# Two square roots of a cross-attention kernel, moved from ScalarE's function to a Newton iteration on VectorE

## The reference

```python
def _l2norm(x, axis=-1):
    n = jnp.sqrt(jnp.sum(x * x, axis=axis, keepdims=True))
    return x / jnp.maximum(n, EPS)                      # EPS = 1e-12
q, k_t, v_t = heads(hidden_states @ W_q), heads(text_ehs @ W_k), heads(text_ehs @ W_v)
probs_t = jax.nn.softmax(jnp.einsum('bhsd,bhtd->bhst', q, k_t) * attn_scale, axis=-1)
text_out = jnp.einsum('bhst,bhtd->bhsd', probs_t, v_t)
attn_scores = jnp.einsum('bhsd,bhnd->bhsn', q, k_ip) * attn_scale
qsem = _l2norm(jnp.einsum('bhst,bte->bhse', probs_t, text_ehs))
ip_n = _l2norm(ip_ehs)
sem = jnp.einsum('bhse,bne->bhsn', qsem, ip_n)
probs_ip = jax.nn.softmax(attn_scores + SEM_SCALE * sem, axis=-1) * spatial_mask[None, None, :, None]
ip_out = jnp.einsum('bhsn,bhnd->bhsd', probs_ip, v_ip)
out = (text_out + ip_out) @ W_out + b_out + residual
```

## Time and profile before

| | before |
|---|---|
| median of 3 runs | 3430.9 us (3430.57 to 3434.68) |
| the profiled execution | 3429.41 us |
| its span | 3427.6 us |
| TensorE, matmuls | 3332.5 us busy, 97% |
| VectorE | 1994.7 us, 58% |
| ScalarE | 1832.7 us, 53% |
| GpSimd | 1089.9 us, 32% |
| mean granted TensorE clock | 0.992 |

### The profile page before, as it was taken

One profiled execution on the slowest core, in us unless ns is written; L12 is line 12 of the kernel. 1 busy time (PEld: TensorE's weight loads), 2 busy tenths in 40 slices (PEclk: granted clock), 3 DMA queues, 4 the chain that ended last, 5 costly groups with the idle time before them and its releaser, 6 DMA issues.

```text
span 3427.6 us, 65589 instructions
## 1 busy us (share of the span) xinstructions
PE 3332.5 (97%) x24736; PEld 2893.1 (84%) x24736; DVE 1994.7 (58%) x5517; ACT 1832.7 (53%) x4006; POOL 1089.9 (32%) x932
## 2 busy tenths in 40 slices
PE   6999999999999999999999999999999999999978
PEld 3888988887888888888888888888888898989755
DVE  4444455556656566565656556665565556555577
ACT  2333343455555555555655555555565556555678
POOL 2111001234332333333433332333423322322368
PEclk8999999999999999999999999999999999999999
DMA  6333823333367332233347422323326532222242
GB/s 185 103 92 71 98 53 92 81 83 83 86 83 101 78 73 68 75 92 82 91 72 72 98 73 68 78 71 106 87 71 75 67 57 49 63 49 53 46 86 54
DMA packets 648781, 271.28 MB, mean 79 GB/s; under 512 B 479666, under 2 KB 599426, under 8 KB 648468
## 3 DMA queue, kind: packets, MB, share of 16 engines
q1 hardware_dynamic: 648468, 267.10, 37.9%
HBM read 187.97 MB, written 79.04 MB: 78 GB/s over the span
## 4 chain that ended last, share of the span: by engine, by line
PE 88%; DVE 5%; ACT 2%; POOL 1%; issue 1%; SPq 1%; DMA 1%; POOLq 0%; ACTq 0%; DVEq 0%
PE acc L1144 9%; PE acc L1137 9%; PE acc L1140 8%; PE acc L1139 8%; PE acc L1145 8%; PE acc L1138 7%; PE score L1104 4%; PE score L1188 4%; PE spare L1188 4%; PE score L1106 4%; PE av L1175 3%; PE av L1179 3%; PE spare L1229 2%; PE spare L1278 2%; PE score L1229 2%; PE score L1278 2%
## 5 line engine op out<-in xcount | busy, mean ns | idle before, releaser
L1355 ACT ACTIVATE prob<-score 128x512 f32<-128x512 f32 x1219 | 729.0, 598 | 1182.5 <-PE score L1106 1177.5
L1775 POOL TENSOR_TENSOR prob_lo<-prob,prob_hi 128x512 fp32r<-128x512 f32 x624 | 812.2, 1305 | 1472.1 <-ACT prob_hi L1358 1471.6
L1137 PE MATMUL acc<-tok_v,prob_hi 128*128 128x300 f32 x2240 | 908.1, 405 | 0.9 <-issue 0.9
L1139 PE MATMUL acc<-tok_lo,prob_hi 128*128 128x256 f32 (+1 forms) x2560 | 760.0, 297 | 0.0
L1144 PE MATMUL acc<-tok_v,prob_lo 128*128 128x278 f32 (+1 forms) x2560 | 745.6, 291 | 0.0
L1358 ACT ACTIVATE prob_hi<-score 128x512 fp32r<-128x512 f32 x1219 | 726.1, 596 | 0.0
L1140 PE MATMUL acc<-tok_lo,prob_hi 128*128 128x256 f32 (+1 forms) x2560 | 719.1, 281 | 0.0
L1145 PE MATMUL acc<-tok_v,prob_lo 128*128 128x256 f32 (+1 forms) x2560 | 717.9, 280 | 0.0
L1138 PE MATMUL acc<-tok_v,prob_hi 128*128 128x256 f32 x2240 | 627.7, 280 | 0.0
L1140 PEld LDWEIGHTS acc<-tok_lo,prob_hi 128*128 128x128 f32 (+1 forms) x2560 | 483.7, 189 | 8.6 <-issue 2.3
L1139 PEld LDWEIGHTS acc<-tok_lo,prob_hi 128*128 128x128 f32 (+1 forms) x2560 | 484.6, 189 | 5.4 <-issue 3.0
(11 more groups left out here) (322 smaller groups left out, 4972.2 us busy)
## 6 DMA issues: line engine op xcount, KB each, us to landing
k_ring<-k_scr SPq DMA_DIRECT2D x160, 384.0 KB
tok_v<-v_scr SPq DMA_DIRECT2D x158, 176.0 KB, 3.3
v_ring<-v_scr SPq DMA_DIRECT2D x160, 148.5 KB, 3.3
ctx_t<-in_ctxT SPq DMA_DIRECT2D x16, 1024.0 KB, 8.8
q_ring<-q_scr SPq DMA_DIRECT2D x160, 96.0 KB
v_scr<-v_stage SPq DMA_DIRECT2D x32, 440.0 KB, 2.5
v_scr<-v_stage SPq DMA_DIRECT2D x36, 330.0 KB, 9.5
tok_stage<-in_ctx SPq DMA_DIRECT2D x32, 256.0 KB, 2.8
```

Source lines behind the costliest of these rows:

```text
L1137: e.matmul(out_a[:, 0:SEG + VCOLS], p_hi, tok_v[0:kk, c, seg, v_lo:v_lo + SEG + VCOLS], start=first, stop=False)
L1139: e.matmul(out_a[:, t0:t0 + SEG], p_hi, tok_lo[0:kk, c, seg * SEG:(seg + 1) * SEG], start=False, stop=False)
L1355: e.activation(prob[:, es, :], bank_s[:, :], ACT.Exp, scale=SCALE)
L1775: e.tensor_tensor(prob_lo[:, ps, :], prob[:, es, :], prob_hi.bitcast(F32)[:, ps, :], ALU.subtract).then_inc(s_low[1], 1)
```

## The change

ScalarE's two `Sqrt` activations are removed. VectorE makes both roots with a helper, `square_root`, called at the start of `ip_scale` and of piece 0 of `fuse_exp`. It clips the input to 1e-37, shifts its bits right by one, subtracts that from a constant (a first guess of 1/sqrt), takes three Newton steps of three instructions each, and multiplies with the input: 1 + 2 + 9 + 1 = 13 instructions, each of which waits for the one before by the semaphore `s_root`. VectorE waits in its own queue for what ScalarE waited for (`out_of_psum` of `ip_norm`, `s_sq`). At the start VectorE writes a zero, and ScalarE takes one exponential of it before all else.

```diff
-        exp_table = sb("exp_table", [P, 1])
+        exp_table = sb("exp_table", [P, 2])
+        root_work = sb("root_work", [P, 2, IP])
...
+            e.wait_ge(s_zero, 1)
+            e.activation(exp_table[:, 1:2], exp_table[:, 0:1], ACT.Exp, scale=0.0)
...
-                elif kind == "ip_norm":
-                    u = s[1]
-                    e.wait_ge(*out_of_psum[job[s]])
-                    e.activation(ip_n[:, 1, :], ip_n[:, 0, :], ACT.Sqrt).then_inc(s_ip_root, 1)
-                    if u == 0:
-                        e.wait_ge(s_mem, 2)
-                        e.activation(exp_table[:], ones_col[:], ACT.Exp, scale=0.0)
-                elif kind == "fuse_root":
-                    u = s[1]
-                    e.wait_ge(s_sq, ST * heads0[head_end[u, HEADS - 1] + 1])
-                    e.activation(small[:, 3, :], sum_sq[:, u % 2, :, :].rearrange("p s h -> p (s h)"), ACT.Sqrt).then_inc(s_f_root, 1)
...
+            def square_root(to, of, clipped, work):
+
+                n = roots_done[0]
+                e.tensor_scalar(clipped, of, TINY, None, ALU.max).then_inc(s_root, 1)
+                e.wait_ge(s_root, n + 1)
+                e.tensor_scalar(to.bitcast(I32), clipped.bitcast(I32), 1, None, ALU.logical_shift_right).then_inc(s_root, 1)
+                e.wait_ge(s_root, n + 2)
+                e.tensor_scalar(to.bitcast(I32), to.bitcast(I32), -1.0, ROOT_START, ALU.mult, ALU.add).then_inc(s_root, 1)
+                n += 3
+                for _ in range(ROOT_STEPS):
+                    e.wait_ge(s_root, n)
+                    e.tensor_tensor(work, to, to, ALU.mult).then_inc(s_root, 1)
+                    e.wait_ge(s_root, n + 1)
+                    e.scalar_tensor_tensor(work, work, -0.5, clipped, ALU.mult, ALU.mult).then_inc(s_root, 1)
+                    e.wait_ge(s_root, n + 2)
+                    e.scalar_tensor_tensor(to, work, 1.5, to, ALU.add, ALU.mult).then_inc(s_root, 1)
+                    n += 3
+                e.wait_ge(s_root, n)
+                e.tensor_tensor(to, to, clipped, ALU.mult).then_inc(s_root, 1)
+                roots_done[0] = n + 1
+                e.wait_ge(s_root, n + 1)
+
+            e.memset(exp_table[:], 0.0).then_inc(s_zero, 1)
...
-                    e.wait_ge(s_ip_root, ip_nth[u] + 1)
+                    e.wait_ge(*out_of_psum[job["ip_norm", u]])
+                    square_root(ip_n[:, 1, :], ip_n[:, 0, :], root_work[:, 0, :], root_work[:, 1, :])
...
-                        e.wait_ge(s_f_root, close0[u] + 1)
+                        e.wait_ge(s_sq, ST * heads0[head_end[u, HEADS - 1] + 1])
+                        square_root(nrm, sum_sq[:, u % 2, :, :].rearrange("p s h -> p (s h)"), small[:, 5, :], n2)
```

More of the change, by code:

```diff
@@ L11 @@
 F32R = mybir.dt.float32r
+I32 = mybir.dt.int32
 BF16 = mybir.dt.bfloat16
@@ L20 @@
 LOWEST = -3.0e38
+TINY = 1.0e-37
+ROOT_START = 1597463007.0
+ROOT_STEPS = 3
 SEM_SCALE = 0.5
@@ L911, in cross_attention_pair @@
         s_out = sem("rows_out_of_psum")
-        s_ip_root = sem("ip_norm_root")
-        s_f_root = sem("fuse_root_done")
+        s_root = sem("root_steps")
+        s_zero = sem("zero_for_exp_table")
         s_f_exp = sem("fuse_exp_done")
@@ L1441, in _ @@
         def _(e):
+            roots_done = [0]
+            def square_root(to, of, clipped, work):
[19 more added lines that the diff above has]
+            e.memset(exp_table[:], 0.0).then_inc(s_zero, 1)
             for x, rows in ((x_in[1], high_rows), (o_t[1], low_rows)):
```

## The result

| | before | after |
|---|---|---|
| median of six runs each, side by side | 3431.3 us | 3442.3 us (3441.5 to 3446.8) |
| ratio, with its 95% interval | | 1.0034 (1.0024 to 1.0044) |
| span of the profiled execution | 3427.6 us | 3440.8 us |

The kernel became slower by 11.0 us. The forecast was 3445 us with a range from 3431 to 3454.

A forecast was written before the change was run, and what follows sets the result against it. TensorE, with matmuls busy for 97% of the span, was taken as the bound. Terms 2.6 + 2.3 + 1.1 + 5.2 - 3.0 + 3.0 + 3.0 = +14.2 us gave a forecast of 3445 us, range 3431 to 3454.

The forecast's parts named there:

- The 2.85 us of the tail: TensorE's stop at the last fuse step (3236 us), counted as winnable once the table loads are gone.
- rival C: VectorE's queue swallows the roots everywhere but at the start, so the kernel gains 7.6 us: 3423 us; chance 7%.
- Steps and lengths: A root is 13 dependent VectorE steps: 3.0 us at a fuse step, 2.6 us for an ip root.
- rival D: A VectorE step costs half of what was taken, so no change: 3429 us; chance 13%.
- 442, 571, 826 us and four other woven fuse steps: First fuse step +2.3 us, second ip_scale +1.1, first woven fuse step -0.1, the other woven ones -0.58 each.
- rival B: At woven fuse steps GpSimd gets in first and holds up L1697; 4.9 us more, 3450 us; chance 20%.
- Third and fourth ip_scale: At 1323 and 2152 us VectorE's whole queue moves by 2.6 us without slack: +2.6 us each.
- The start: The root before L1503 lies on the path, TensorE waits for L1509 and nothing covers it: +2.6 us.
- The last fuse step: At 3236 us GpSimd holds up five steps, L1695 comes 5.0 us late: +3.0 us, bounds 0 and 5.0.
- TensorE's clock: Three new stops of 2.3 to 2.6 us, two followed by half clock at about 1.5 us each: +3.0 us.
- The table switch: On ScalarE a load takes 1.283 us, the next activation 0.01 us after; the page's 2.66 us per switch was rejected.

The follow-up runs named there:

- x3: The kernel after with one clip in place of the 13 root steps, so that no square root is taken: 3423.3 us, 0.9976 of before.
- y1: The kernel after with 1/root used directly, two Newton steps, the ip root made in `ip_norm` and the fuse root spread over three steps: 3424.3 us, 0.9984 of before.
- x1: The kernel after with the eight fuse roots back on ScalarE, only the four ip roots on VectorE: 3438.9 us, 1.0021 of before.
- x6: The kernel after with only the last unit's fuse root back on ScalarE, with its two table loads: 3437.9 us, 1.0019 of before.
- x5: The kernel after with the `prob_lo` subtractions of the tail's first nine chunks on VectorE instead of GpSimd: 3445.2 us, 1.0042 of before.
- r0: The kernel before, run again unchanged: 3431.2 us, ratio 1.0005.

## Why the prediction was right, point by point

*The frame was right.* TensorE's idle time was the currency, and the waits the loads cause, 1.23 us at six places, were the whole gain to be had there; x3 shows 7.5 us for 6 x 1.23. The 2.85 us of the tail were not to be had in full: with the chain left out, 1.5 of them are won. That rival C (the loads decide, 3423 us) was wrong follows from x3 too: the queue swallows the roots only when the chain is left out, or shortened and spread as in y1.

*Steps and lengths.* 13 x 0.23 = 3.0 and 13 x 0.20 = 2.6 us were forecast, 2.99 and 2.57 us were measured. The two forms that no row had shown (scalar-tensor-tensor and the integer shift) take 0.20 and 0.18 us at 128x40: the reading by the nearest row held, and rival D (half of that) falls.

*442, 571, 826 us and four other woven fuse steps.* Forecast 2.3, 1.1, -0.1 and -0.58, measured 2.4, 1.1, -0.13 and about -0.61. Here each number was a new end in VectorE's queue less the moment at which TensorE wants the result, and that is why they came out. The sixth woven step went by rival B, +0.12 instead of -0.58.

*Third and fourth ip_scale: mis-sized, 2.6 forecast, 1.75 and 1.5 measured.* The step that failed is "GpSimd held L1509 up before and holds up the third new instruction now". GpSimd's start was taken from the old clock. But that subtraction follows ScalarE's exponential, and without the loads at this place (one pair, 2.6 us) it comes sooner: at 2155.53 us on the new clock, which is 2149.7 on the old one, where it stood at 2152.20. It is over before the root begins. L1531 takes 0.17 us instead of 1.25, and 2.57 - 1.08 = 1.5. At 1327 us it is the same, and another 0.23 us go where L1623 starts 0.34 us behind L1591 instead of 0.11. The loads of `ip_norm` were not free after all: they had pushed a GpSimd operation onto a VectorE one. The two rows of before:

```profile
2152.20 1.29 POOL L1775 TENSOR_TENSOR prob_lo<-prob,prob_hi 128x512 fp32r<-128x512 f32 x1 [6.29 <-ACT prob_hi L1358]
2152.27 1.25 DVE L1509 TENSOR_TENSOR w_text<-ctx_t,ip_n 128x16 f32<-128x16 f32 x1
```

*The start: 2.6 forecast, 3.3 and 3.7 measured.* The mechanism is the one named, with the wait for L1531 as its sign. The chain alone costs what was forecast, as x1 shows: 2.6 us with full clock behind the stop. What comes on top in after is the half clock, 3.87 against 2.42 us for the same eight matmuls, which the forecast had put at nothing here; part of it is made up by 60 us. At 100 us the five traces with this stop are 1.8 to 3.7 us behind, and before's own two traces differ by 1.2 there, so the tenths are chance.

*The last fuse step: +3.0 forecast with bounds 0 and 5.0; 2.9 in the trace, 3.4 to 4.6 by x6's ratios and medians.* Five steps held up for 1.2 us each were forecast. L1718 was to be 5.0 us late and is 4.8 (3250.07, less the lag of 7.6 us, is 3242.5), and x5 shows that GpSimd is the cause. The 3.0 itself was a choice between the bounds, not worked out, so that it fits is in part luck. Here the Trainium skill's rule ("SBUF — State Buffer", section "Who interferes with whom") was borne out by the trace of after and by x5: 1.2 us a step with GpSimd at work, 0.20 without.

*TensorE's clock: +3.0 forecast for two of three mid-kernel stops at 1.5 us each.* The price was right (1.4 to 1.5 us behind 446 us, 1.6 behind 1334), the share was not. Behind the stop at 446 us four of six traces have the fall, behind those at 1327 and 2155 us (1.76 and 1.52 us, where 2.3 to 2.6 were forecast) one in ten (after twice, x1, x5, x6). As an estimate from these counts and prices the three stops cost 1.3 us on average, not 3.0. In the first trace of after there was none in mid-kernel; its total came near the forecast because the tail lost 2.5 us more than forecast. That is a right total by two errors that cancel, and as r0 shows, it is of a size that before varies by itself. By the medians, which that chance doesn't touch, the change cost 11.0 us of the 14.2 forecast; the terms that were too large are the clock and the two ip_scale steps. Which stops pull the clock down in a given execution stays open.

*The table switch.* The prediction put a switch at the 1.283 us of its row. x3, with no load left, won the 1.23 us a site that this had given, so the row was the right one to take. The Trainium skill ("ScalarE: Activation LUTs", section "What ACT_TABLE_LOAD costs") has the same 1283 ns for the load itself, and 1380 ns of drain with it, 2.66 us in all; the trace agrees on the load and shows no drain (the next activation starts 0.01 us behind it). By the page's total, as an estimate, the six woven stops would have been longer by some 2.5 us each.

## What to carry to other kernels

A function moved to an engine that is idle on average still lengthens one unbroken stretch of its queue: count the steps times the start-to-start time of dependent ones (0.20 us at 128x4 and 0.23 at 128x40 here), and set the end against the moment at which the next reader wants what stands behind it. Placed where that engine waits anyway, the same 13 instructions cost 0.4 us or less. When loads or waits are removed on one engine, move the starts of all that follows from it, GpSimd's too, before saying which VectorE instruction it will hold up. And the choice needn't be the same at every place: the version with the lowest median kept ScalarE's root at two of eight fuse steps. Last, take more than one trace of before when single microseconds are at stake: here the first one was 2.5 us luckier in the tail than most.

## What the runs showed of the hardware that was not expected

- In a chain of dependent VectorE instructions beside back-to-back GpSimd subtractions, one step got through per subtraction: 1.17 to 1.21 us each, five in a row, with 0.20 us before and behind. It made no difference whether the form had two inputs or was an integer shift with one (1.20 us against 0.18 at 1252.57 us).
- TensorE's granted clock isn't the same in each execution of one program: behind the same stop of 2.2 us it was 1.00 in one trace and 0.79 in the next over 444 to 452 us, and in the tail 0.88 against 0.76. That moves single stretches by 1.4 to 3 us, more than the 1.23 us that a pair of table loads cost at a woven step; only the comparison of many runs, or of stretches at full clock, tells a change of this size.
